# Second attention: the row maximum enters the score banks as a ScalarE copy instead of as a matmul

## The reference, cut to what matters

```
q = rms_norm((x @ wq).reshape(B, L, 16, 128), q_norm_w)
k = rms_norm((x @ wk).reshape(B, L, 4, 128), k_norm_w);  v = x @ wv
k_ctx, v_ctx = the same from the context (1601 rows), without rotation
q, k = rotated by position (cos, sin)
scores = q . [k_ctx, k] * 128**-0.5 + causal mask
probs = softmax(scores);  out = probs . [v_ctx, v];  out @ wo
```

## Time and profile before

| | us |
|---|---|
| median of 3 runs | 2540.25 (2534.80 to 2542.76) |
| the profiled execution's own time | 2537.91 |
| its span, first to last instruction | 2535.9 |
| first score matmul L1622 to last | 568.4 to 1825.9 |
| the second attention, all 16 turns | about 568 to 1835 |

### The profile page before, as it was taken

How to read it: one execution, slowest core, us unless ns; L and a number is a source line. 1 busy time by engine, 2 the same in 40 slices (tenths; PEclk the granted TensorE clock), 3 DMA queues, 4 the chain that set the end, 5 groups by cost and what they waited for, 6 DMA issues and landing times.

```text
span 2535.9 us, 53694 instructions
## 1 busy us (share of the span) xinstructions
PE 2422.8 (96%) x19523; PEld 1716.4 (68%) x19584; DVE 1721.2 (68%) x3346; ACT 1480.1 (58%) x3291; POOL 1388.0 (55%) x944
## 2 busy tenths in 40 slices
PE   7989999989999999999999999999989899999997
PEld 4777777757777777777777777777755544444434
DVE  5455757677787878778787877878721467666546
ACT  2235444446556665556655565555511488888897
POOL 1044645526666766667666676667710478778500
PEclk9989999989999999999999999999989999999999
DMA  5122222220001000010000100000320200000100
GB/s 188 62 88 83 86 83 85 86 108 17 1 17 48 18 17 2 17 48 18 2 17 18 47 18 1 18 17 1 136 105 13 63 19 26 24 14 24 55 3 18
DMA packets 42362, 108.73 MB, mean 43 GB/s; under 512 B 5060, under 2 KB 25928, under 8 KB 36936
## 3 DMA queue, kind: packets, MB, share of 16 engines
q1 hardware_dynamic: 40312, 102.28, 12.1%
q0 software_dynamic: 768, 2.10, 0.3%
q10 hardware_dynamic: 1008, 0.79, 0.1%
HBM read 99.78 MB, written 4.98 MB: 41 GB/s over the span
## 4 chain that ended last, share of the span: by engine, by line
PE 77%; DVE 11%; ACT 5%; issue 4%; POOL 1%; DMA 1%; another core or an unknown queue 0%; DVEq 0%; SPq 0%; ACTq 0%; POOLq 0%
PE psum L1600 9%; PE psum L513 6%; PE psum L515 6%; PE psum L514 6%; PE psum L1687 4%; PE psum L1622 4%; PE psum L1640 4%; PE psum L2736 4%; PE psum L1637 4%; PE psum L1638 4%; PE psum L2100 3%; PE psum L2703 3%; ACT l_p L2539 3%; PE psum L2669 2%; PE psum L393 2%
## 5 line engine op out<-in xcount | busy, mean ns | idle before, releaser
L1299 POOL TENSOR_TENSOR xn<-xn,l_p 128x512 f32<-128x512 f32 (+1 forms) x400 | 638.8, 1597 | 177.1 <-ACT l_p L1342 160.0
L1432 DVE TENSOR_TENSOR l_plo<-l_p,l_phi 128x512 fp32r<-128x512 f32 (+1 forms) x464 | 403.6, 871 | 62.3 <-ACT l_p L1342 38.0
L2539 ACT ACTIVATE l_p<-psum 128x1024 f32<-128x1024 f32 x416 | 397.7, 1036 | 54.0 <-PE psum L2703 49.5
L1341 ACT ACTIVATE l_phi<-psum 128x512 fp32r<-128x512 f32 (+1 forms) x464 | 279.6, 603 | 219.4 <-PE psum L515 140.0
L1483 DVE TENSOR_REDUCE l_mx<-psum 128x1 f32<-128x512 f32 (+2 forms) x512 | 305.3, 617 | 36.1 <-PE psum L1687 36.1
L2514 POOL TENSOR_TENSOR l_rs<-l_ms,half_power 128x32 f32<-128x32 f32 x45 | 244.4, 5431 | 68.7 <-DVE l_ms L2564 58.7
L1342 ACT ACTIVATE l_p<-psum 128x512 f32<-128x512 f32 (+1 forms) x464 | 281.6, 607 | 0.0
L2736 PE MATMUL psum<-l_p,l_vs 64*32 64x256 f32 x6656 | 252.3, 378 | 7.3 <-issue 3.2
L1622 PE MATMUL psum<-l_m,l_ones 128*128 128x512 f32 (+1 forms) x464 | 233.5, 503 | 0.0
L1600 PE MATMUL psum<-l_w,l_ctx 128*128 128x256 f32 (+1 forms) x832 | 217.0, 384 | 0.8 <-DVE l_vlo L1476 0.8
L1687 PE MATMUL psum<-l_kThi,l_qThi 128*128 128x512 f32 (+2 forms) x512 | 197.9, 427 | 4.9 <-DVE l_mx L1483 2.5
(11 more groups left out here) (410 smaller groups left out, 5191.8 us busy)
## 6 DMA issues: line engine op xcount, KB each, us to landing
w_stage<-in_L_w_dram SPq DMA_DIRECT2D x76, 384.0 KB, 3.0
l_w<-in_L_w_qkv_dram SPq DMA_DIRECT2D x16, 1024.0 KB, 5.0
l_ct<-in_ctx_tiles_dram SPq DMA_DIRECT2D x52, 128.0 KB, 2.2
c_T<-in_ctx_T_dram SPq DMA_DIRECT2D x4, 1601.0 KB, 8.0
l_ctx<-in_ctx_T_dram SPq DMA_DIRECT2D x4, 1601.0 KB, 6.8
c_N<-in_ctx_dram SPq DMA_DIRECT2D x4, 1536.0 KB
s_wg<-in_L_gate_dram SPq DMA_DIRECT2D x4, 1024.0 KB, 11.9
s_wu<-in_L_up_dram SPq DMA_DIRECT2D x4, 1024.0 KB, 14.2
```

Source lines behind the costliest of these rows:

```text
L1299: g_.tensor_tensor(l2_acc[k][0:r, :], first[0:r, :], l2_p[c % 3][0:r, :], ALU.add)\
L1432: v.tensor_tensor(l2_plo[c % 3][0:r, :], l2_p[c % 3][0:r, :], l2_phi[c % 3][0:r, :].bitcast(F32), ALU.subtract)\
L2539: act.activation(l3_p[ring(odd, c)][:, :], psum[:, (c % 2) * 2 * BANK:(c % 2 + 1) * 2 * BANK], ACT.Exp, scale=float(D3) ** -0.5).then_inc( ...
```

## The change

A score bank is no longer started by a matmul. ScalarE copies a finished tile into the bank (`seeds`), and the three score matmuls, all of them without `start`, add to what stands there. In detail:

- L1622 is gone from all 464 steps. The mask matmul adds too.
- `tops` on VectorE, after the maximum, writes `l2_diag`: for each head a 128x128 diagonal block with the maxima (128x512). `shifts` on VectorE is gone.
- `maxima` on TensorE is now one matmul of 512 columns, a matrix of minus ones (`l2_minus`) times `l2_diag`, so that bank 7 holds minus the maximum in all partitions.
- `shift` on ScalarE (places 25 and 7) copies bank 7 to `l2_shift`, 128x512.
- `seeds` on ScalarE copies `l2_shift` into the bank of step c + 3 as soon as the exponentials of step c have been read from it; it waits for ScalarE's own semaphore. The first three steps of the first turn have a starting matmul instead.
- ScalarE's order at a place changes: the exponentials come first, then the projection copies, then the seed; before, the projection copies came first.
- `l2_e` counts three events to a step instead of two, and TensorE's scores wait for the seed.
- Two memsets of `l2_m` on GpSimd are gone. No transfer is added, removed or moved.

```diff
+            def shift(g, k):
+                act.wait_ge(l2_mT, g * TB + (k + 1))
+                act.activation(l2_shift[:, k, :].bitcast(F32), bank(7), ACT.Copy)\
+                    .then_inc(l2_md, 2 if k == 0 and isinstance(g, int) and g == 0 else 1)
+            def seeds(g, c, n):
+                def seed(c):
+                    return act.activation(bank(c % 3), l2_shift[:, STEPS[c][0], :].bitcast(F32), ACT.Copy)
+                if c == NS - 3 or c > NS - 3 and n is None:
+                    return
+                act.wait_ge(l2_e, g * (3 * NS) + (3 * c + 2))
...
+                seed(c + 3 if c < NS - 3 else c + 2 - NS).then_inc(l2_e, 1)
+                if c == NS - 1:
+                    seed(2).then_inc(l2_md, 1)
...
             def turn(g, slot, n):
                 new = 1 - slot
                 for c in range(NS):
+                    at, step = ahead(c, 2, g, n)
+                    if at is not None:
+                        exp(at, step)
...
+                    if n is not None and c == M_AT + 1:
+                        shift(n, 0)
+                    if g is not None and c == M1_AT + 1:
+                        shift(g, 1)
                     if at is not None:
-                        exp(at, step)
+                        seeds(at, step, n if c + 2 < NS else None)
...
             def tops(g, k):
-                v.tensor_reduce(l2_mx[:, k * REP:(k + 1) * REP], l2_mx4[:, k * REP:(k + 1) * REP, :], AX.X, ALU.max)\
-                    .then_inc(l2_top, 1)
+                mx = l2_mx[:, k * REP:(k + 1) * REP]
+                dve_steps.then(v, v.tensor_reduce(mx, l2_mx4[:, k * REP:(k + 1) * REP, :], AX.X, ALU.max))
+                v.tensor_tensor(l2_diag[:, k, :].rearrange("p (h n) -> p h n", h=REP),
+                                ident[:, :].unsqueeze(1).to_broadcast([P, REP, P]),
+                                mx.unsqueeze(2).to_broadcast([P, REP, P]), ALU.mult).then_inc(l2_top, 1)
-            def shifts(g, slot, k):
...
+                opened = c < 3 and isinstance(g, int) and g == 0
+                if opened:
+                    pe.wait_ge(l2_top, 1)
+                elif c == 2:
+                    pe.wait_ge(l2_md, g * NSHIFT + 2)
+                else:
+                    pe.wait_ge(l2_e, g * (3 * NS) + 3 * (last + 1) - (0 if c >= 3 else 3 * NS))
...
-                pe.matmul(dst, l2_ones[:, 0:even], l2_m[slot][:, k, :], start=(j < MC + k), stop=False)
-                three(pe, dst, (l2_kThi[slot][:, keys], l2_kTlo[slot][:, keys]),
-                      (l2_qThi[slot][:, k, :], l2_qTlo[slot][:, k, :]), False, True).then_inc(l2_s, 1)
+                pe.matmul(dst, l2_kThi[slot][:, keys], l2_qThi[slot][:, k, :], start=False, stop=False, skip_group_check=True)
+                pe.matmul(dst, l2_kThi[slot][:, keys], l2_qTlo[slot][:, k, :], start=False, stop=False, skip_group_check=True)
+                pe.matmul(dst, l2_kTlo[slot][:, keys], l2_qThi[slot][:, k, :], start=False, stop=True, skip_group_check=True)\
+                    .then_inc(l2_s, 1)
...
             def maxima(g, k):
                 pe.wait_ge(l2_top, g * TB + (k + 1))
-                pe.transpose(bank(7, P)[0:REP, :], l2_mx[:, k * REP:(k + 1) * REP], ident[:, :]).then_inc(l2_mT, 1)
+                pe.matmul(bank(7), l2_minus[:, :], l2_diag[:, k, :], start=True, stop=True).then_inc(l2_mT, 1)
```

More of the change, by code:

```diff
@@ L1102, in program @@
         TURNS = B * KH
+        NSHIFT = TB + 1
         def l2_slot(s):
@@ L1141, in program @@
         l2_vhi, l2_vlo, l2_kThi, l2_kTlo, l2_qThi, l2_qTlo, l2_m = zip(l2_slot(0), slot1)
+        l2_shift, l2_diag = l2_m
         l2.close()
@@ L1341, in exp @@
                 act.activation(l2_phi[c % 3][0:r, :], src, ACT.Exp).then_inc(l2_e, 1)
-                act.activation(l2_p[c % 3][0:r, :], src, ACT.Exp).then_inc(l2_e, 1)
+                act.activation(l2_p[c % 3][0:r, :], src, ACT.Exp)\
+                    .then_inc(l2_e, 2 if c == NS - 3 or c > NS - 3 and last_turn(g) else 1)
+            def shift(g, k):
[8 more added lines that the diff above has]
+                act.wait_ge(l2_e, g * (3 * NS) + (3 * c + 2))
+                if c == NS - 2:
+                    act.wait_ge(l2_md, n * NSHIFT + 1)
+                elif c < NS - 3 and STEPS[c + 3] == (1, 0):
+                    act.wait_ge(l2_md, g * NSHIFT + NSHIFT)
+                elif c == 0 and isinstance(g, int) and g == 0:
+                    act.wait_ge(l2_md, 1)
+                seed(c + 3 if c < NS - 3 else c + 2 - NS).then_inc(l2_e, 1)
+                if c == NS - 1:
+                    seed(2).then_inc(l2_md, 1)
             def products(g, k):
@@ L1616, in scores @@
                     pe.wait_ge(l2_far, SHARED[at][1] + 1)
[L1617 removed]
+                opened = c < 3 and isinstance(g, int) and g == 0
[5 more added lines that the diff above has]
+                    pe.wait_ge(l2_e, g * (3 * NS) + 3 * (last + 1) - (0 if c >= 3 else 3 * NS))
                 dst = bank(c % 3)[0:even, :]
                 keys = slice(a, a + even)
+                if opened:
+                    pe.matmul(dst, l2_minus[:, :], l2_diag[:, k, :], start=True, stop=True)
                 if j == MC + k:
[L1621 to L1624 removed]
+                    pe.matmul(dst, identb[:, :], causal_T[:, :, :].rearrange("p h n -> p (h n)"), start=False, stop=False,
+                              skip_group_check=True)
+                pe.matmul(dst, l2_kThi[slot][:, keys], l2_qThi[slot][:, k, :], start=False, stop=False, skip_group_check=True)
+                pe.matmul(dst, l2_kThi[slot][:, keys], l2_qTlo[slot][:, k, :], start=False, stop=False, skip_group_check=True)
+                pe.matmul(dst, l2_kTlo[slot][:, keys], l2_qThi[slot][:, k, :], start=False, stop=True, skip_group_check=True)\
+                    .then_inc(l2_s, 1)
             def values(g, slot, c):
@@ L1694, in prepare @@
                         if k == 0:
-                            need(pe, l2_md, n * TB)
+                            need(pe, l2_md, n * NSHIFT)
                         else:
```

35 lines of the change are left out of this document (9 added, 26 removed).

## The result

The changed kernel takes 2511.43 us (median of 4 runs, 2509.76 to 2512.53) against 2537.77 for the kernel before on the same chip: ratio 0.9898, 95% interval 0.988 to 0.9917. It is 26 us faster; 60 were forecast. The direction held, and the time lies just inside the slow end of the range (2440 to 2512); the size did not hold.

The account below looks back on a forecast made before the run. TensorE was taken to bound the attention, VectorE close behind. Savings of 0.70 + 0.35 + 0.93 + 0.68 + 1.5 = 4.16 us a turn, 62.4 for 15, less 1.5 in the last, gave 2478 us; range 2440 to 2512.

Parts of the forecast that it names:

- TensorE's price: Each removed starting matmul costs TensorE 0.233 us start to start, not 0.503; 6.76 us for one turn.
- cost 0: ScalarE's seeds cost nothing: up to 1 us behind, catching up 0.6 us a place; only the high keys' copy excepted.
- my 0.12: ScalarE's wait for its own exponential before each seed, priced at 0.12 us from such a wait on VectorE.
- The lead of two places: ScalarE works ahead: TensorE needs the seed of place c two places later, about 4 us of lead.
- The keys' copy: At places 16 and 19 TensorE arrives 0.23 us earlier and waits for ScalarE's high-half key copy: 0.25 us each.
- Places 3 to 8: VectorE works through without pause; of TensorE's possible 1.40 us, between 0 and 0.67 gained, 0.35 taken.
- Places 17 to 28: TensorE could save 2.80 us; VectorE's idle 2.68 less 1.19 of key-transpose waits limits the gain to 1.5 us.
- The last turn: Prepares nothing; GpSimd's sums keep 1.65 us a step, ScalarE has 1.70: no gain, 1.5 us lost.
- The turn's length: A sign in the changed profile: a turn of about 75 us.
- the second rival: VectorE and GpSimd hold each other up more; places 3 to 8 and 17 to 28 bring nothing: 2507 us, chance 0.18.
- `l_plo`'s average: Sign over all l_plo: below 0.95 us means the main case, 1.0 or more the second rival.
- That rule: VectorE with two SBUF inputs and GpSimd lock shared ports; l_plo and l2_diag held up more often in a shorter turn.

Follow-up runs that it names:

- experiment 6: Changed kernel with each ScalarE seed cut to 8 of 512 columns, shift by the row maximum left out: 2499.26 us, ratio 0.9856.
- Experiments 2: Changed kernel with VectorE's second x addition of place 5 moved ahead of the rotation's sum of that place: 2513.86 us, ratio 0.9894.
- 10: Changed kernel with the two output products and x additions at places 2 and 3 instead of 3 and 5: 2503.03 us, ratio 0.9866.
- experiment 3: Changed kernel with GpSimd's running sums cut to 8 of 512 columns, softmax denominators left out: 2452.02 us, ratio 0.9654.
- experiment 7: Changed kernel with VectorE's l2_diag cut to 8 of 512 columns after the first turn's: 2504.04 us, ratio 0.9875.
- experiment 9: Changed kernel with GpSimd's sum waiting for VectorE's l_plo of the same step, for steps 21 to 28 only: 2497.86 us, ratio 0.9843.
- experiment 1: Changed kernel with ScalarE's old order inside a place (projection copies, then exponentials, then seed): 2541.72 us, ratio to before 1.0.

## Why the prediction was right in direction and wrong in size

**TensorE's price: right.** The forecast took 0.233 us a step from the timeline and not 0.503 from the page. The places where nothing waits fell by 0.23 to 0.25 (18, 22, 23, 25, 27), and the surcharge after a full-fp32 projection moved to L1648.

**ScalarE: right as to the bound, wrong at "cost 0".** The seed takes 0.60 us, as I took it. Its own wait is shorter than my 0.12:

```profile
1107.89 0.59 ACT L1341 ACTIVATE l_p<-psum 128x512 f32<-128x512 f32 x1
1108.52 0.60 ACT L1352 ACTIVATE psum<-l_m 128x512 f32<-128x512 f32 x1
```

The exponential ends at 1108.48, the seed starts at 1108.52: 0.04 us. The lead of two places held too, with 6 waits for seeds. But I looked only at what TensorE takes from ScalarE. VectorE takes from it as well: the copy of the values at place 3, ahead of the rotation, started 9.08 us after place 0's scores before; after the change it starts at 8.73 in the turns without a jump ahead and at 9.86 behind a jump, although TensorE is 0.73 us further by then. The forecast said that ScalarE falls behind by up to 1 us and catches up at 0.6 us a place; behind the jump it falls behind by 1.4 (the first copy of the turn at 1.53 in place of 0.10) and still lacks 1.13 at place 3. I had no term for the jump. It makes 1.26 us in six turns, and experiment 6, with short seeds, leaves 0.13 of that.

**The keys' copy: right.** 0.25 us more at 16 and at 19: its waits went from 8.7 to 16.1 us over 30, 0.25 each, and places 17 and 20, in which the search waits for the copy, kept their length (2.45 to 2.48, 2.45 to 2.44) where those beside them fell by 0.23.

**Places 3 to 8: the step that failed.** Of the 2.22 us a turn that are missing (4.16 forecast, 1.94 measured), 1.11 are lost here and 0.84 at places 17 to 28. The forecast said -0.35 and got +0.76: +0.24 in the turns without a jump ahead, +1.38 behind one. I wrote that VectorE "works through this stretch without pause" and took half of the shift's time as a gain. I had the stretch's end in view (l_plo of place 8), and missed the earlier meeting: bank 7 at place 6. Before, `maxima` stood at 19.57 us after place 0's scores and the x addition ended at 19.44 on average, a spare of 0.1; the shift, which goes, comes behind it and gives nothing there. TensorE could now be there 1.5 us earlier; the x addition ends at 19.14, 0.3 us earlier, and behind a jump at 20.41, 1.0 later. Experiments 2 and 10 show that the place of that meeting is not the cause and VectorE's work is; experiment 3 shows that 2.1 us of the stretch go with GpSimd's sums.

**Places 17 to 28: the limit was right, its height was not.** -1.5 was VectorE's idle time less two waits. VectorE is saturated there as forecast (28.27 of 29.0). What I held constant was its work: the diagonal tile (0.72 us of place 24 by experiment 7; I had taken 0) and l_plo's lengthening (0.871 us on average before, 0.987 after; 1.08 us of the stretch by experiment 9). The two overlap, since either cut brings place 24 to 2.31. The forecast had 2 of the 12 `l_plo` lengthen in its rival and none in its sum; one more did (3 instead of 2 above 1.2 us).

**The last turn** lost 1.0 us against 1.5 forecast, and in part for another reason. Without the sums its 26 steps take as long in the kernel before as with them (48.8 us), so GpSimd did not pace it there, as I had it; in the changed kernel they take 49.8, 48.2 without the sums and 46.7 with small seeds. ScalarE sets the pace there in the main, as forecast.

**The turn's length.** The 79 us that I gave for a turn, and the 75 that followed, contain the short last one; a full turn takes 80.5, so that the forecast stood for 76.3. The sum used savings alone and is not touched by it.

So the second rival was the case in the main, and its 2507 the better number: VectorE and GpSimd hold each other up more, both critical stretches bring nothing together (-0.35 - 1.50 forecast, +0.76 - 0.66 = +0.10 measured). It had one `l_plo` more lengthened at 3 to 8 and two at 17 to 28; by the rows it was 1.5 (1.2 to 2.8 in a turn) and one. `l_plo`'s average, the sign that I had named, does not decide: 0.987 us lies between its two marks (0.95 and 1.0). And part of the nearness of 2507 is luck, since about 8 us of the lost gain are the jump's, which no rival had. I gave it 0.18 with the argument that both start on the same event and so mostly keep their order. The rows before place 24 show that they keep it no longer once VectorE is behind: a saturated VectorE takes its l_plo late, when the sum of the same step is already running, and experiment 9, which forces the order, brings the 1.78 us back to 0.68. The Trainium skill (SBUF — State Buffer, "SBUF: two separate sides") describes the pair of ports as an exclusive lock that the second one waits for; the trace agrees, with l_plo at 0.69 us when it goes first and up to 1.79 when it goes second (1.78 behind a sum that started 0.26 us ahead), and 687 ns on average without sums. That rule was quoted in the forecast and priced in a rival; it should have been in the sum.

What is still open: how the 2.1 us of places 3 to 8 divide between VectorE held up by the sums and ScalarE's exponentials held up by them, and what the change would bring if ScalarE had no jump. No run here separates the first two or tries the last. Nor is it only the exponentials' place that lays the jump bare: experiment 1 has the copies first again, and its turns behind a jump are still 0.68 us longer than the others (80.98 and 80.30).

## What to carry to other kernels

Taking time from the engine that sets the pace shortens the cover of all others: for every stretch, add up the next engine's work at its longest seen durations, not its mean, and look for every resource that the faster engine will now ask for earlier, banks included. Two engines that interfere do it more as they fill up, so their work is not a constant of the kernel; a run with one of them emptied, before and after the change, tells what the interference costs. And where VectorE and GpSimd are released by one event, an explicit order can win in one stretch and lose in the next: try it by stretch. An average over turns can hide two kinds of them: look at single turns, and at the head of a loop ask what stands first behind the jump, an instruction that had to wait anyway or one that was ready.

## What was not expected of the hardware

- A sum on GpSimd and a two-input instruction on VectorE lengthen each other: `l_plo` from 0.69 to as much as 1.79 us, the sums from 1.27 to as much as 2.43; emptied sums made the 464 `l_plo` 687 ns on average in both kernels, against 987 and 871.
- At a loop's jump ScalarE of the changed kernel stood idle for 2.2 to 2.4 us with nothing to wait for; in the kernel before, at the same jump, the wait for TensorE's projection (2.07 us in both kinds of turn) hid it.
- ScalarE writes a 128x512 tile from SBUF into PSUM in 0.60 us, the same as it needs from PSUM to SBUF (0.624 and 0.606 on average). A seed that waits for the exponential just ahead of it starts 0.04 us after its end, where VectorE showed 0.12.
- Not shown: that TensorE adds to what ScalarE wrote into the 461 banks. The changed kernel relies on it, but a softmax does not change when all scores of a row shift alike (experiment 6 leaves the shift out), so a right output tells of the adding only where banks begun by a matmul and seeded banks meet in one row, in the first tile of the first turn. No run here reads a bank.
